# Decoder layer on one core: where the last batch's maxima units stand

## The reference, cut to what matters

```
x = x + self_attn(layernorm(x))              # scores masked, softmax over the queries
q = layernorm(x) @ Wq + bq;  k, v = ctx @ Wk + bk, ctx @ Wv + bv
x = x + softmax(q k^T / sqrt(8)) v @ Wo + bo # 16 heads, 256 x 256 scores each
s = layernorm(x) @ Wr + br;  two best experts per row, softmax of their two scores
x = x + sum over the two: weight * (relu(n @ W1[e] + b1[e]) @ W2[e] + b2[e])
```

## Time and profile before

| what | value |
|---|---|
| median of 3 runs | 325.09 us (324.94, 325.09, 328.87) |
| the profiled execution | 324.41 us |
| its span | 322.7 us, 5945 instructions |
| granted TensorE clock, mean | 0.973 of full speed |
| busy: TensorE, VectorE, ScalarE, GpSimd | 275.5, 192.9, 183.7, 149.3 us |

### The profile page before, as it was taken

The page is one execution under the profiler, slowest core; times in us unless marked ns, Lnnn a source line. Parts: engine busy times, 40 slices in busy tenths (PEclk is TensorE's granted clock), DMA queues, the critical chain, the costliest instruction groups (busy, mean ns, idle before and its releaser), DMA issues.

```text
span 322.7 us, 5945 instructions
## 1 busy us (share of the span) xinstructions
PE 275.5 (85%) x2035; PEld 202.8 (63%) x2035; DVE 192.9 (60%) x459; ACT 183.7 (57%) x513; POOL 149.3 (46%) x212
## 2 busy tenths in 40 slices
PE   6789999999989899797999796635468979989994
PEld 2577777877777578454745353421148979978993
DVE  3777666376458885976377273785017766556561
ACT  1669858387737664465277977424444554544441
POOL 7991290127130200720047895187922545544485
PEclk9999999999999999999999999776799999999999
DMA  7900015530590010001067370001663015420301
GB/s 231 216 3 3 2 30 63 65 41 20 145 211 26 17 34 2 5 0 46 6 187 241 83 202 0 3 30 57 167 207 124 11 30 190 171 81 11 98 18 50
DMA packets 27291, 25.24 MB, mean 78 GB/s; under 512 B 3866, under 2 KB 20332, under 8 KB 27260
## 3 DMA queue, kind: packets, MB, share of 16 engines
q1 hardware_dynamic: 24462, 22.46, 26.4%
q0 software_dynamic: 1216, 1.61, 1.7%
q10 hardware_dynamic: 1584, 0.80, 0.9%
HBM read 12.49 MB, written 4.80 MB: 54 GB/s over the span
## 4 chain that ended last, share of the span: by engine, by line
PE 53%; DVE 14%; POOL 13%; issue 10%; DMA 4%; ACT 3%; another core or an unknown queue 2%; SPq 1%; POOLq 0%; ACTq 0%; DVEq 0%
PE ps L902 6%; PE ps L828 5%; PE ps L935 5%; PE ps L829 5%; PE ps L830 5%; PE ps L947 4%; PE ps L983 3%; PE ps L909 2%; POOL px L712 2%; DVE mneg L1566 2%; POOL w_lo L689 2%; PE ps L1020 2%; POOL w_raw L683 2%; DMA w_in<-in_L_attn_W_qkv 2%; PE ps L937 2%
## 5 line engine op out<-in xcount | busy, mean ns | idle before, releaser
L1286 ACT ACTIVATE p<-ps,negmax 128x256 f32<-128x256 f32 (+1 forms) x128 | 52.7, 426 | 25.2 <-DVE negmax L1537 24.7
L1566 DVE TENSOR_REDUCE mneg<-ps 128x2 f32<-128x512 f32 x64 | 42.7, 684 | 17.7 <-PE ps L983 17.6
L1316 ACT ACTIVATE px<-ps 128x512 f32<-128x512 f32 x64 | 35.3, 601 | 20.1 <-PE ps L1005 14.5
L1537 DVE TENSOR_REDUCE negmax<-ps 128x2 f32<-128x512 f32 (+1 forms) x48 | 32.9, 686 | 19.6 <-PE ps L904 12.5
L1740 DVE SCALAR_TENSOR_TENSOR hid_lo<-ps,hid_hi 128x512 fp32r<-128x512 f32 x42 | 28.9, 690 | 23.6 <-ACT hid_hi L1359 20.1
L1359 ACT ACTIVATE hid_hi<-ps 128x512 fp32r<-128x512 f32 x42 | 25.1, 598 | 30.3 <-PE ps L830 26.7
L613 POOL TENSOR_SCALAR tmp<-mv 128x2 f32<-128x2 f32 x8 | 1.8, 230 | 78.1 <-DVE mv L1561 77.8
L720 POOL DMA_INDIRECT ys<-yrow,xr x26 | 25.4, 977 | 24.5 <-DVE yrow L1746 17.2
L983 PE MATMUL ps<-k_st,q_mem 128*128 128x256 bf16 x128 | 25.2, 285 | 8.5 <-DVE mneg L1566 8.2
L1005 PE MATMUL ps<-q_mem,k_st 128*128 128x512 bf16 x64 | 23.8, 414 | 8.4 <-ACT px L1316 5.0
L1272 ACT CAST t_hi<-ps 128x512 fp32r<-128x512 f32 x32 | 18.8, 592 | 19.5 <-PE ps L830 18.5
(11 more groups left out here) (269 smaller groups left out, 762.2 us busy)
## 6 DMA issues: line engine op xcount, KB each, us to landing
ovw<-w_hi SPq DMA_DIRECT2D x10, 256.0 KB
ovw<-w_lo SPq DMA_DIRECT2D x10, 256.0 KB
w_raw<-in_L_ffn_W SPq DMA_DIRECT2D x2, 1024.0 KB, 8.2
xs<-pad SPq DMA_DIRECT2D x1, 1716.0 KB, 10.0
k_st<-k_part SPq DMA_DIRECT2D x12, 128.0 KB
q_mem<-q_part SPq DMA_DIRECT2D x48, 32.0 KB
w_last<-in_L_ffn_W SPq DMA_DIRECT2D x4, 256.0 KB, 7.2
w_late<-in_L_ffn_W SPq DMA_DIRECT2D x4, 256.0 KB, 5.1
```

The source lines that it names most:

```text
L1286: last = act.activation(dst, bank[:, n * i:n * i + n], ACT.Exp, bias=negmax[:, kt, h:h + 1], accum_out=psums[:, kt, h:h + 1])
L1316: act.activation(px[:, (g // 2) % 2, c0:c0 + 512], ps[:, score_banks[k], :], ACT.Exp, scale=SCALE_X).then_inc(s_px, 1)
L1537: dve.tensor_reduce(dst, ps[:, k % 3, :].rearrange("p (h q) -> p h q", h=n), AX, ALU.max, negate=True).then_inc(s_max, 1)
L1566: dve.tensor_reduce(mneg[:, qt, :].rearrange("p (r g) -> p r g", r=2)[:, :, g], ps[:, max_bank[("MX", b, u)], :].rearrange("p (h k) -> p h ...
```

## The change

`MX_BESIDE` gets two more entries: slots 6 and 7 of batch 2's scores take two units each. So units 8 to 11 of batch 3 stand beside the scores, and units 12 to 15 in the long slot.

```
-        MX_BESIDE = (2, 2, 1, 1, 1, 1)
+        MX_BESIDE = (2, 2, 1, 1, 1, 1, 2, 2)
```

## The result

| what | before | after |
|---|---|---|
| median of 11 runs each, same chip | 324.94 us | 327.68 us (327.09 to 330.43) |
| ratio, 95% interval | | 1.0094 [1.0064, 1.0125] |
| the profiled execution | 324.41 us | 328.07 us |
| its span, mean granted clock | 322.7 us, 0.973 | 326.3 us, 0.957 |

A forecast was written before the change was run, and what follows sets the result against it. No single engine bounds the passage from batch 2's scores to batch 3's, but a chain through TensorE, VectorE, GpSimd and a DMA. +0.44 + 1.79 - 0.27 = +1.96 us on the 325.09 median gives 327.05, stated as 327.0; range 323.6 to 329.2.

The forecast's parts named there:

- The forecast and its sign: Whole kernel: slower by 1.96 us, to 327.0 us (own range 326.2 to 328.2); chance 0.52.
- Step 1: TensorE beside batch 2's scores: two units ahead of the router's product delay it and VectorE's score copy by 0.44 us.
- Step 2: VectorE behind best_two: ranks wait for the twelfth unit's eviction, +1.79 us more; 2.23 in all carried through to positions and scatter.
- Step 3: VectorE behind batch 2's residual: four evictions fewer return only 0.27 us at the turn, since the router's second product holds it.
- Step 4: Batch 3's scores onward: delay passes to the end; the unexplained 5.44 us stop at 223.78 keeps its length, starting later.
- The fixed moment: Rival at batch 3's fourth pair of scores: stop ends at a fixed moment, swallowing the delay, 325.1 us; chance 0.18.
- its other branch: Same place in batch 3: the stop instead ends with GpSimd's scatters, 2.23 us later, giving 327.3 us, inside the forecast.
- VectorE as the bound: Rival: ranks do not wait, delays shrink to about nothing; 324.8 us, or 322.65 without a product ahead of the turn; chance 0.07.
- The stop didn't vanish: Judges the rival that batch 3's stop at 223.78 vanishes, being due to how engines meet: 321.6 us; chance 0.09.
- The clock's rival: Rival on TensorE: clock falls longer, two more batch 3 output products at the lower level, 1.7 us more, 328.8; chance 0.14.

The follow-up runs named there:

- e1: The kernel before with two extra maxima units in slot 6 only, ten beside the scores; ratio 1.0014 to the kernel before.
- e2: The kernel before with two extra maxima units in slot 7 only, behind the pick of the experts; ratio 1.0106 to the kernel before.
- e3: The changed kernel with its twelfth unit in bank 3, so the ranks need not wait for that eviction; ratio 1.0022 to the kernel before.
- e4: The kernel before with all four moved units in slot 5, ahead of the transposes; ratio 1.0044 to the kernel before.
- e5: The kernel before with GpSimd's first scatter behind the normalisation of batch 2 instead of ahead of it; ratio 1.0033.
- e8: The kernel before with four units moved to slot 5, all scatters behind batch 2's normalisation, and TensorE's stream 40 matmuls longer at the start; 326.79 us.
- e6: The kernel before with four units moved to slot 5 and GpSimd's first scatter behind batch 2's normalisation; 326.64 us, ratio 1.0043.
- e10: The kernel before with places worked out directly behind the ranks and five scatters ahead of batch 2's norm, the row broken into 5, 3 and 4; 321.86 us, 0.9884.
- e11: The kernel before with one line: GpSimd waits for the first eight scatters' landing before issuing the last four; 321.49 us, ratio 0.9878.
- e12: The kernel before with places computed early, five scatters ahead of batch 2's norm, and four extra units in slot 5; ratio 0.9891.

## Why the prediction was right or wrong

**The forecast and its sign** held: slower by less than 1%, 327.68 against 327.0. Its sum was 1.96 us and the interval of the ratio says 2.1 to 4.1, so it was too small, by 0.8 at the median.

**Step 1 (+0.44)** was right to the hundredth: from the transposes to the router's product it was 2.00 us and is 2.44. The copy moved by 0.67 because the transposes themselves came 0.23 later.

**Step 2 (+1.79 more for the ranks)** was right in place and kind: +1.69, two reductions directly behind `best_two`, `mneg` as releaser, the third with a gap ahead. e1 and e2 show that this place is the cost. What did not hold is the sentence that followed it, that 2.23 can be carried through to the positions because "all of it has the same content in both kernels". The content is the same and the duration isn't: from the ranks to the positions it took 7.62 us in place of 7.14. Those 0.48 lie at the transposes that ran at 1.2 GHz. e2 and e3, which have the reductions in a row behind `best_two`, show the longer transposes too (1.12); e1 and e4, which haven't, show 0.66. The lower clock is not itself due to the wait: in twelve of the fourteen traces it falls between 204.6 and 208.1, whatever the order (206.2 in before), and in e1 and e5 at 213.4 to 213.5. The change moves the transposes from 204.06 to 206.44, past that fall; how often an execution pays this can't be said from one trace of each kernel. Second, "the ranks' wait" was only half of the mechanism up to the division: e3 took the wait away and left 0.88 of 1.70 in VectorE's queue, though e3's times are near those of before.

**Step 3 (-0.27)** was near: second copy behind the positions 7.36 before, 7.16 after, so 0.20 came back. VectorE stood idle for 2.38 us there, as forecast ("about 2"). That the four reductions behind the residual had been covered by GpSimd's norm and the router's product is what makes moving them nearly worthless: the change paid 2.36 us at the ranks for these 0.20.

**Step 4 (a stop of fixed length)** is the step whose picture failed. The sum needed a shift of the same size in and out and got 2.79 in, 3.17 out. But the stop isn't a fixed length: it is 5.45 to 7.33 us in e5 to e8, its beginning goes with the score products and its end with the row of scatters. That this term came out near nothing was luck: the change moves both by 2.8 us, and the prediction did not know that the end hung on the scatters, which it had only as a rival. Where only the scores come earlier (e6), the gain of 0.9 vanishes in it.

**The rivals.** The fixed moment of 325.1 is out; its other branch, that the stop ends with the scatters, is what happened, at the 327.3 it was priced at plus the clock. VectorE as the bound is out as a whole (e2), though e3 shows it as the second half of the delay. The stop didn't vanish here, but e10 and e11 show that it can, and that this is worth 3.0 and 4.0 us by their medians, not the whole 5.44. In e11 ScalarE still idles 0.97 us at that place, and from the copy to the first expert tile 4.31 us are gained. The clock's rival was right in kind: 1.2 GHz from 206.1 to 226.6 without a break, across 5.12 us of idle time, where before had full speed from 209.6 to 213.1. The Trainium skill, TensorE: Matmul & The Clock Gate, table "Why this matters for your kernels", advises against idle gaps between bursts of matmuls. The trace agrees for that long gap; the fall at 206.1 came ahead of it, with no idle time above 1.81 us since 197, and in before at 206.2 too. The price that rows show is 0.48 us, at the transposes, and not where the rival had it, at output products of batch 3. What the sum below leaves unexplained may be the clock's too, but no run shows it.

**The sum with what was measured**, in the two traces: 0.23 (transposes later) + 0.44 + 1.69 + 0.48 (lower clock) - 0.20 = 2.64 at the turn; + 0.15 to the first scores, + 0.38 at the stop, + 0.06 to the first expert tile, + 0.37 behind it = 3.60 of span. The 0.23, 0.15, 0.38 and 0.37 aren't explained. The 0.15 and the 0.38 don't look like the change's: e1 and e4, whose first scatter and turn come as far behind the copy as in before or sooner, have them too (4.77 and 4.72 us from the turn to the first exponential against 4.58, stops of 5.80 and 5.83 against 5.43). By the medians (2.74) only 0.10 us lies behind the turn's 2.64, so most of what lies there may belong to these two executions alone.

## What to carry to other kernels

Work that looks free to move must be placed by what stands behind it on each engine: two reductions directly behind the pick of the experts cost more than four that were covered by another engine's path gave back. When a bank is reused, see who next waits for its eviction, and where that eviction now stands in its engine's queue. A stop that the profile puts down to nobody is worth an experiment of one line before anything around it is tuned: here a pause in a long row of indirect DMAs was worth 1.2%, and none of the orders of the maxima units that were tried gained anything that the times show.

## What the runs showed of the hardware that was not expected

- A row of 11 or 12 indirect DMAs on GpSimd, mostly 0.96 us each and 0.30 apart, goes with 5.4 to 7.3 us in which TensorE's completions don't reach ScalarE, though neither waits for those DMAs in the program. With rows of at most 7 (e10 to e12) ScalarE idled there for 1.0 to 1.4 us.
- In that time the trace shows the matmuls as done (the output product from 222.90 to 224.14 in before) and the waiting engine's releaser as "remote", while the semaphore's update comes at 229.16. Here the modelled end of a matmul did not say when its completion arrived.
- The same kernel spends very different times at the lower clock: before, in the 29 runs beside e1 to e4 that the ratios use, some 19 to 35 us by each run's mean granted clock ((1 - clock) x 2 x span), with times of 324.5 to 329.2 us. An edit of a few tenths is below that, and one profile of each kernel can't show it. A single fall ahead of the copy, from 196.3 to 199.8 in e5, went with 1.58 us more from the transposes to the copy.
- A missing matmul record looks like a longer wait: from the turn to the first recorded score product it is 4.5 us in e1 to e4, where the first product's record is missing, and 3.9 to 4.1 in the others; to the first exponential they differ by 0.23 us at most.
